# Naming, per engine, only the latest awaited stage, and none twice, in a one-core Mamba and transformer kernel

## The chip, the cores and the metric

The kernel runs on one core of one Trainium2 chip. The metric is the device time of that core in microseconds (us), as the median of the runs shown. Each engine of the core (TensorE, here PE; VectorE, DVE; ScalarE, ACT; GpSimd, POOL; SyncE, SP) takes its own list of instructions in order, and the engines meet through semaphores: an instruction adds to one when it has ended, and another engine waits until it has reached a value.

## The reference, cut to what matters

The input is x[4, 1024, 128]. It goes through a bidirectional Mamba block with a layer norm and a residual, then through a transformer of six layers with local attention (16 heads of 64, windows of 32 tokens, each looking back one window) and a gated feed-forward part, and the first block's sum is added at the end.

```
xc = silu(conv(x @ W_in));  dt = softplus(...);  h = h*exp(dt*A) + dt*xc*B;  y = (h*C).sum + xc*D
per layer:  q,k,v = x @ Wqkv;  q,k normed, scaled, rotated;  x = x + softmax(8*q.k, local) @ v @ Wo
            x = x + (a * gelu(gate)) @ W2 + b2,   a,gate = layernorm(x) @ W1 + b1
```

## The kernel before, in words

The program has two blocks, one after the other. `mamba` (lines 175 to 722) takes 8 sequences (4 batches in 2 directions) with 16 states each; a state's step is a scan on DVE (L658), a product on POOL (L696) and a sum on PE (L439). `transformer` takes 6 layers of 32 tiles of 128 tokens, and 8 chunks of 512 tokens for the feed-forward part, 48 chunks and 192 tiles in all.

In both blocks the order of the work is written out by hand. `PE_ORDER`, `ACT_ORDER`, `DVE_ORDER` and `POOL_ORDER` (and `MAMBA_PE` and its like) list the stages of one iteration as (lag, which tile, name); `sequence` unrolls them, so that each engine has one flat list of (name, k), and a stage is a function that emits the waits and the instructions of one entry. One iteration of the transformer is one chunk with its four tiles. No queue is reordered.

Every stage name has its semaphore in `done`, and `after` (L972 for the transformer, L225 for the Mamba block) puts one wait per producer named, whatever was waited for before:

```python
def after(eng, *producers):
    for name, k in producers:
        eng.wait_ge(done[name], k + 1)
```

So `output` on PE waits for the four stages `copy_mixed0` to `copy_mixed3`, all of them ACT's, and for the reader of the PSUM bank that it takes (`turn_free`), often an ACT stage too; `score` waits for four `copy_heads` and `exponent`, all ACT's; `mix` waits for `turn_probs`, `copy_rows`, the two shift DMAs (`shifted_back`) and the readers of four banks. `ff_added` waits for `x_low` and `x_ready`, which DVE raises one after the other.

The program has 9211 such instructions in the transformer (PE 3203, ACT 3036, DVE 1972, POOL 804, SP 196) and 2013 in the Mamba block (PE 370, ACT 718, DVE 489, POOL 292, SP 144). Stages call first, as a rule, for the data they read (`("normed..")` in `head_turn`, `("square..")` in `squares`, `("sc..")` in `read_out`) and then for the buffer they overwrite.

Other waits are written out with `wait_ge` where they belong to no stage (weights, tables, DMA landings, the steps within a stage).

Of the kernel before, what the change touches and what calls it, by code (L numbers as in the profile page):

```python
# [164 lines left out]
def mamba(nc, xn, resid, c_rows, kept, kept_stored, weights, hbm):  # L165
    win, wtap, wx, wdt, wout, packed, ident, pick, ln, ones_mean, centring, eps_col = weights
    with ExitStack() as ctx:
# [38 lines left out]

        COUNT, done = {}, {}
# [689 lines left out]

def transformer(nc, ctx, consts, xa, xb, resid, kept, kept_stored, hbm, out, stored):
# [72 lines left out]

    def after(eng, *producers):  # L972
        for name, k in producers:
            eng.wait_ge(done[name], k + 1)

    def ff_added(eng, chunk):

        eng.wait_ge(x_low, chunk + 1)
        eng.wait_ge(x_ready, chunk + 1)
# [22 lines left out]
    with nc.Block() as block:  # L1002
        @block.sync
        def _(sp):
# [22 lines left out]
            def load_w2(l):  # L1027
                if l >= 2:
                    ff_added(sp, CHUNKS * l - 1)
                sp.dma_start(w2[:, l % 2], hbm["w2"][l]).then_inc(w2_loaded, 16)  # L1030
                sp.dma_start(lp[:, l % 2], hbm["lp"][l]).then_inc(w2_loaded, 16)
# [42 lines left out]
        def _(pe):  # L1074
# [6 lines left out]
            def in_variance(chunk):  # L1081
                after(pe, ("in_square", chunk))
                bank = turn_free("in_variance", chunk)
                pe.matmul(bank, ones_mean[:, :], in_work(chunk), start=True, stop=True).then_inc(done["in_variance"], 1)

            def turn_free(name, k, i=0):
                last = TURNS[name, k, i][1]
                if last and last[0] == "ff_output":
                    ff_added(pe, CHUNKS + last[1])
                elif last and last[0] in ("fold0", "fold1"):  # L1090
                    pe.wait_ge(vo_copied, 4 * last[1] + 2 * int(last[0] == "fold1") + last[2] + 1)
                elif last and last[0] == "mix":
                    after(pe, (f"copy_mixed{last[2]}", last[1]))
                elif last and last[0] == "in_variance":
                    pe.wait_ge(done["in_rstd"], 2 * last[1] + 1)
                elif last:
                    after(pe, (TURN_READERS[last[0]], last[1]))
                return turn_bank(name, k, i)

            def fold(two):  # L1100
                def stage(l):

                    pe.wait_ge(wvo_loaded, 32 * l + 32)
                    banks = [turn_free(f"fold{two}", l, odd) for odd in range(2)]
# [7 lines left out]
            def project(part):  # L1112
                def stage(tile):
                    l, t, odd = place(tile)
                    after(pe, ("rest", tile))
                    if t == 0:
                        pe.wait_ge(wqk_low, 2 * l + part + 1)
                    if tile == 0:
                        pe.wait_ge(x_ready, 2)
                    if part:  # L1120
                        after(pe, ("cosines0", tile), ("sines0", tile))
                    elif tile:
                        after(pe, ("cosines1", tile - 1), ("sines1", tile - 1))
# [18 lines left out]
            def row_turn(tile):  # L1142
                l, t, odd = place(tile)
                ff_added(pe, CHUNKS * l + t // CHUNK_TILES)
                bank = turn_free("row_turn", tile)
                pe.transpose(bank[:, 0:P], shifted(xa, t * P, P), ident[:, :]).then_inc(done["row_turn"], 1)  # L1146

            def score(tile):
                l, t, odd = place(tile)
                after(pe, ("copy_heads0", tile), ("copy_heads1", tile), ("copy_heads2", tile), ("copy_heads3", tile))  # L1150
                if tile:
                    after(pe, ("exponent", tile - 1))
                else:
                    pe.wait_ge(const_loaded, 64)
                    pe.wait_ge(x_ready, CHUNKS)
# [47 lines left out]
            def mean(chunk):  # L1203
                after(pe, ("add_output", CHUNK_TILES * chunk + CHUNK_TILES - 1))
                bank = turn_free("mean", chunk)
# [3 lines left out]
            def variance(chunk):  # L1209
                after(pe, ("square", chunk))  # L1210
                bank = turn_free("variance", chunk)
                pe.matmul(bank, ones_mean[:, :], work[:, :], start=True, stop=True).then_inc(done["variance"], 1)  # L1212

            def hidden_part(name, first):
                def part(k):
                    lo, m = HIDDEN_PARTS[k]

                    def stage(chunk):
                        after(pe, ("rest_high", chunk))
                        if chunk % CHUNKS == 0:  # L1220
                            pe.wait_ge(w1_low, chunk // CHUNKS + 1)
                        bank = turn_free(f"{name}{k}", chunk)
# [7 lines left out]
            def ff_output(chunk):  # L1230
                after(pe, *[(f"product{k}", chunk) for k in range(3)])
# [3 lines left out]
                bank = turn_free("ff_output", chunk)  # L1235
# [13 lines left out]
        def _(act):  # L1249
# [27 lines left out]
            def round_high(tile):  # L1277
                l, t, odd = place(tile)
                ff_added(act, CHUNKS * l + t // CHUNK_TILES)
                if tile >= 2:  # L1280
                    after(act, ("project1", tile - 2))
                act.copy(xs_parts[:, odd, 0, :], shifted(xa, t * P, P)).then_inc(done["round"], 1)

            def square(part):
                def stage(tile):
                    after(act, (f"project{part}", tile))
                    if part:
                        after(act, ("squares0", tile))
                    elif tile:
                        after(act, ("squares1", tile - 1))  # L1290
# [3 lines left out]
            def inverse_norm(tile):  # L1294
                odd = tile % 2
                after(act, ("guard", tile))
                if tile >= 2:
                    after(act, ("normed0", tile - 2), ("normed1", tile - 2))
# [5 lines left out]
            def copy_heads(c):  # L1304
                def stage(tile):
                    name = f"copy_heads{c}"
                    after(act, (f"head_turn{c}", tile))
                    bank = turn_bank(f"head_turn{c}", tile).rearrange("p (j n) -> p j n", j=4)
                    if tile >= 2:
                        after(act, ("score", tile - 2))  # L1310
# [5 lines left out]
            def copy_rows(tile):  # L1316
                after(act, ("row_turn", tile))
                if tile >= 2:
                    after(act, ("mix", tile - 2))
# [3 lines left out]
            def exponent(tile):  # L1323

                after(act, ("find_max", tile))
                if tile >= 2:
                    after(act, ("turn_probs", tile - 2))
# [5 lines left out]
            def copy_mixed(w):  # L1333
                def stage(tile):
                    after(act, ("mix", tile))
                    if tile >= 2:
# [429 lines left out]
```

## Time and profile before

| what | value |
|---|---|
| median of 3 runs | 3916.18 us (3915.42 to 3918.15) |
| profiled execution, its own time | 3923.24 us |
| its span, first to last instruction | 3921.5 us |
| granted TensorE clock, mean | 0.979 |
| PE busy | 3716.7 us, 95% |
| DVE, POOL, ACT busy | 3307.3, 3178.6, 3035.4 us |

The profile is of one execution. A busy PE means that a matmul was under way by a modelled end. PEld is the weight load of a matmul, which overlaps the matmul before. The event-semaphore instructions are not counted as busy; the view of one source line lists them under PEldq, ACTq, DVEq and so on, where a long one is a wait that it held. "issue" as releaser means that no wait that the profile shows ended the idle time.

### The profile page before, as it was taken

How to read it: one execution, taken by the hardware profiler on the slowest of the kernel's cores; microseconds unless marked ns; L12 is line 12 of the kernel's file. 1: busy time of each engine (PE TensorE's matmuls, PEld its weight loads, DVE VectorE, ACT ScalarE, POOL GpSimd, SP SyncE). 2: the span in 40 equal slices, each digit the busy share in tenths (PEclk: the TensorE clock that was granted, in tenths of full speed). 3: DMA queues.
4: the chain of work that ended last, by engine and by line, in shares of the span. 5: the costliest groups of instructions: out<-in, count | busy, mean ns of one | idle time of the engine just before them, and what ended most of it. 6: DMA issues, size and time to landing. Idle time of an engine off the chain costs nothing.

```text
span 3921.5 us, 115027 instructions
## 1 busy us (share of the span) xinstructions
PE 3716.7 (95%) x45104; PEld 2578.1 (66%) x45104; DVE 3307.3 (84%) x3327; ACT 3035.4 (77%) x7250; POOL 3178.6 (81%) x2370
## 2 busy tenths in 40 slices
PE   7999999988799999999999999999999999999997
PEld 2444444433377777777777777777777777777775
DVE  2999999999688887888878887888878888788885
ACT  7776667666488887888878887888878887888885
POOL 2787778877688888888888888888888888888883
PEclk8999999999899999999999999999999999999999
DMA  1122222222100000000000000000000000000001
GB/s 60 71 81 76 76 74 73 81 73 84 43 21 7 20 7 6 21 7 20 7 10 18 7 20 6 11 17 7 21 6 10 18 7 20 7 11 6 7 7 47
DMA packets 62307, 115.01 MB, mean 29 GB/s; under 512 B 10820, under 2 KB 37320, under 8 KB 61648
## 3 DMA queue, kind: packets, MB, share of 16 engines
q1 hardware_dynamic: 61776, 107.66, 8.3%
q8 instruction: 366, 6.00, 0.6%
q14 instruction: 165, 1.35, 0.1%
HBM read 90.32 MB, written 4.72 MB: 24 GB/s over the span
## 4 chain that ended last, share of the span: by engine, by line
PE 66%; issue 3%; ACT 2%; POOL 1%; DVE 0%; POOLq 0%; ACTq 0%; DVEq 0%
PE ps L1199 17%; PE ps L1127 13%; PE ps L1188 9%; PE ps L1138 8%; PE ps L1175 6%; PE ps L1224 5%; PE ps L1237 3%; PE ps L1160 2%; PE ps L1206 1%; PE ps L1212 1%; PE ps L1146 1%; POOL resid L1604 1%; POOL resid L1626 0%; ACT prob L1329 0%; ACT mixed L1338 0%
## 5 line engine op out<-in xcount | busy, mean ns | idle before, releaser
L1604 POOL TENSOR_TENSOR resid<-resid,sq 128x1024 f32<-128x1024 f32 x384 | 910.3, 2376 | 2.1 <-DVE sq L1459 2.1
L696 POOL TENSOR_TENSOR read<-state,c_row 128x1024 f32<-128x1024 f32 x256 | 646.2, 2540 | 178.7 <-DVE state L658 99.4
L1626 POOL TENSOR_TENSOR resid<-resid,rnorm 128x1024 f32<-128x1024 f32 x384 | 725.0, 1904 | 17.8
L1199 PEld LDWEIGHTS ps<-mixed,w_vo 128*128 128x128 f32 x6144 | 710.9, 193 | 26.7 <-issue 18.6
L1199 PE MATMUL ps<-mixed,w_vo 128*128 128x128 f32 x6144 | 720.2, 276 | 3.2 <-ACT mixed L1338 3.2
L1127 PE MATMUL ps<-w_qk,xs_parts 128*128 128x512 f32 x2304 | 635.6, 412 | 37.4 <-issue 19.4
L1329 ACT ACTIVATE prob<-ps,stat 128x64 f32<-128x64 f32 x3072 | 650.8, 382 | 0.7 <-DVE stat L1479 0.5
L1459 DVE TENSOR_TENSOR sq<-ps,rope_l 128x1024 f32<-128x1024 f32 x384 | 462.5, 1205 | 103.9 <-ACT sq L1291 103.7
L1472 DVE TENSOR_TENSOR resid<-ps,rope_l 128x1024 f32<-128x1024 f32 x384 | 464.9, 1211 | 82.5 <-ACT sq L1291 75.2
L1291 ACT ACTIVATE sq<-ps 128x1024 f32<-128x1024 f32 x384 | 395.6, 1030 | 154.2 <-PE ps L1127 121.4
L1127 PEld LDWEIGHTS ps<-w_qk,xs_parts 128*128 128x128 f32 x2304 | 414.0, 192 | 152.5 <-issue 74.1
L1338 ACT COPY mixed<-ps 128x512 f32<-128x512 f32 x768 | 399.4, 602 | 135.9 <-PE ps L1188 135.7
L439 PE MATMUL mamba_ps<-read,ident 128*128 128x512 f32 x1024 | 498.9, 623 | 3.0 <-POOL read L696 3.0
L1633 POOL TENSOR_TENSOR prob<-prob,stat 128x1024 f32<-128x1024 f32 x192 | 365.7, 1905 | 160.7 <-DVE stat L1490 160.7
L1436 DVE TENSOR_REDUCE ssq<-sq 128x16 f32<-128x1024 f32 x384 | 465.6, 1213 | 5.5 <-ACT sq L1291 0.9
L658 DVE TENSOR_TENSOR_SCAN state<-decay,mamba_ps 128x1024 f32<-128x1024 f32 x192 | 430.5, 2270 | 10.8 <-ACT decay L591 6.0
L1138 PE MATMUL ps<-ident,resid 128*128 128x128 f32 x3072 | 421.4, 276 | 14.6 <-ACT w_vo L1273 13.1
L1138 PEld LDWEIGHTS ps<-ident,resid 128*128 128x128 f32 x3072 | 351.8, 141 | 86.1 <-issue 66.3
L439 PEld LDWEIGHTS mamba_ps<-read,ident 128*128 128x128 f32 x1024 | 190.8, 198 | 230.3 <-issue 219.9
L1313 ACT COPY q_t<-ps 128x512 f32<-128x512 f32 x384 | 234.5, 611 | 117.3 <-PE ps L1138 114.6
L1175 PE MATMUL ps<-k_t,q_t 64*32 64x64 f32 (+1 forms) x24576 | 291.7, 224 | 32.2 <-issue 32.1
L591 ACT ACTIVATE decay<-dt,neg_a 128x1024 f32<-128x1024 f32 x256 | 280.2, 1142 | 49.6 <-DVE state L658 49.4
(149 smaller groups left out, 6038.1 us busy)
## 6 DMA issues: line engine op xcount, KB each, us to landing
c_row<-c_rows SPq DMA_DIRECT2D x128, 512.0 KB, 3.6
rows_back<-rows SPq DMA_DIRECT2D x192, 48.0 KB, 1.9
w_stage<-w_qk_hbm SPq DMA_DIRECT2D x12, 512.0 KB, 4.6
vo_stage<-w_v_hbm SPq DMA_DIRECT2D x6, 512.0 KB, 4.0
vo_stage<-w_o_hbm SPq DMA_DIRECT2D x6, 512.0 KB, 5.0
rows_back<-rows SPq DMA_DIRECT2D x192, 16.0 KB, 1.8
xn<-x_hbm SPq DMA_DIRECT2D x4, 512.0 KB, 5.7
kept<-resid SPq DMA_DIRECT2D x8, 256.0 KB, 4.2
```

The source lines that it names most:

```text
L439: last = pe.matmul(y_ps[h][:, c, :], ident[:, :], read[:, h, g % 2, cols(c)], start=False, stop=n == LAST)
L696: pool.tensor_tensor(read[:, h, g % 2, :], state[:, h, g % 2, :], c_row[:, g % C_AHEAD, :], ALU.mult).then_inc(done[f"rd{h}"], 1)
L1127: last = pe.matmul(ps[:, A + c, :], xs_parts[:, odd, xpart, :], w_qk[:, wpart, cols], start=k == 0, stop=k == 2)
L1138: last = pe.transpose(bank[:, j * P:(j + 1) * P], qk[:, tile % 2, col:col + P], ident[:, :])
L1175: last = pe.matmul(ps[w * WINDOW:(w + 1) * WINDOW, S + h, first:(a + 1) * 2 * WINDOW], q_t[rows_h, odd, a, w * WINDOW:(w + 1) * WINDOW], k ...
L1199: last = pe.matmul(bank[:, 0:P], w_vo[:, l % 2, head_at(place_h), :], mixed[:, odd, place_h, :], start=place_h == 0, stop=place_h == HEADS ...
L1329: last = act.activation(prob[:, tile % 2, place_h, :], score_ps[:, place_h, :], ACT.Exp, bias=stat[:, tile % 2, 0, place_h:place_h + 1])
L1436: dve.tensor_reduce(ssq[:, tile % 2, part * HEADS:(part + 1) * HEADS, 0], sq[:, 0, :].rearrange("p (h d) -> p h d", d=HEAD_DIM), AX_X, ALU ...
L1459: dve.tensor_tensor(sq[:, 1 + part, :].rearrange("p (h s d) -> p h s d", s=2, d=HEAD_DIM // 2), swapped, table(part, 1, tile).rearrange("p ...
L1472: dve.tensor_tensor(qk[:, tile % 2, part * INNER:(part + 1) * INNER].rearrange("p (h d) -> p h d", d=HEAD_DIM), heads_ps.rearrange("p (h d ...
L1604: pool.tensor_tensor(qk[:, tile % 2, cols], qk[:, tile % 2, cols], sq[:, 1 + part, :], ALU.add).then_inc(done[f"rotated{part}"], 1)
L1626: pool.tensor_tensor(heads, heads, norms, ALU.mult).then_inc(done[f"normed{part}"], 1)
```

## The change

One helper, `latest`, gets all stages that a call of `after` names. It keeps, for each engine that produces some of them, the one that stands last in that engine's list, drops it if the waiting engine has already waited for that place or a later one, and notes the place. The stages that are left are waited for in the order PE, ACT, DVE, POOL. Places are looked up in the flat lists.

```diff
+def places(orders):
+    return {stage: (side, n) for side, order in enumerate(orders) for n, stage in enumerate(order)}
+
+def latest(met, eng, stages, places):
+    asked = {}
+    for side, n, stage in sorted((*places[stage], stage) for stage in stages if stage[1] >= 0):
+        asked[side] = n, stage
+    asked = {side: x for side, x in asked.items() if x[0] > met.get((eng.engine, side), -1)}
+    met.update({(eng.engine, side): n for side, (n, _) in asked.items()})
+    return [stage for _, stage in asked.values()]
```

In the Mamba block the calls stay where they are; DMA stages (`cd`, `cst`) are waited for as before, ahead of the others:

```diff
             for name, k in producers:
-                if k >= 0:
+                if k >= 0 and name in ("cd", "cst"):
                     eng.wait_ge(c_spread[k % C_AHEAD] if name == "cd" else done[name], COUNT[name, k])
+            for stage in latest(met, eng, [x for x in producers if x[0] not in ("cd", "cst")], stands):
+                eng.wait_ge(done[stage[0]], COUNT[stage])
```

In the transformer `after` uses `latest` too, `ff_added` goes and is replaced by `after(eng, x_of(chunk))`, which names `in_norm` or `add_ff` and waits for `x_ready` alone, and in each stage on PE, ACT and DVE the separate calls become one (on DVE `cosines` and `add_ff` keep two). A PE stage now puts the bank's reader into the same call:

```diff
-            def turn_free(name, k, i=0):
+            def freed_by(name, k, i=0):
                 last = TURNS[name, k, i][1]
                 if last and last[0] == "ff_output":
-                    ff_added(pe, CHUNKS + last[1])
-                elif last and last[0] in ("fold0", "fold1"):
+                    return [("add_ff", last[1])]
+                if last and last[0] in ("fold0", "fold1"):
                     pe.wait_ge(vo_copied, 4 * last[1] + 2 * int(last[0] == "fold1") + last[2] + 1)
...
+            def turn_free(name, k, *producers):
+                after(pe, *producers, *freed_by(name, k))
+                return turn_bank(name, k)
...
             def head_turn(c):
                 def stage(tile):
-                    after(pe, (f"normed{c // 2}", tile))
-                    bank = turn_free(f"head_turn{c}", tile)
+                    bank = turn_free(f"head_turn{c}", tile, (f"normed{c // 2}", tile))
...
             def mix(tile):
-                after(pe, ("turn_probs", tile), ("copy_rows", tile))
+                after(pe, ("turn_probs", tile), ("copy_rows", tile), *[x for w in range(WINDOWS) for x in freed_by("mix", tile, w)])
                 shifted_back(pe, tile)
-                banks = [turn_free("mix", tile, w) for w in range(WINDOWS)]
+                banks = [turn_bank("mix", tile, w) for w in range(WINDOWS)]
...
             def output(tile):
                 l, t, odd = place(tile)
-                after(pe, *[(f"copy_mixed{w}", tile) for w in range(WINDOWS)])
                 if t == 0:
                     pe.wait_ge(vo_copied, 4 * l + 4)
-                bank = turn_free("output", tile)
+                bank = turn_free("output", tile, *[(f"copy_mixed{w}", tile) for w in range(WINDOWS)])
```

No computing instruction, no DMA, no buffer and no place in an order is changed.

## Rows read from the trace of the kernel before

**Rows 1.** The page: busy time of each engine, share of the span, instructions.
```profile
PE 3716.7 (95%) x45104; PEld 2578.1 (66%) x45104; DVE 3307.3 (84%) x3327; ACT 3035.4 (77%) x7250; POOL 3178.6 (81%) x2370
```

**Rows 2.** Busy us by stretch: PE, PEld, DVE, ACT, POOL; then clock, DMA share, GB/s.
```profile
0.00:1022.00 1022.00, 933.54 (x2658) 422.14 (x2658) 908.47 (x517) 683.78 (x957) 746.83 (x305) 0.95 0.22 75
1022.00:3921.50 2899.50, 2783.13 (x42448) 2155.93 (x42446) 2398.82 (x2810) 2351.58 (x6294) 2431.76 (x2066) 0.99 0.05 13
```

**Rows 3.** View of one line: count, shortest/median/longest ns, first and last start.
```profile
L974 PEldq EVENT_SEMAPHORE  x3111: 51/51/3930, 1033.5 to 3910.6; - x195
...
L974 DVEq EVENT_SEMAPHORE  x1957: 21/21/3454, 1038.6 to 3906.3; - x196
...
L229 PEldq EVENT_SEMAPHORE  x365: 51/51/6463, 19.1 to 1006.2; - x183
```

**Rows 4.** Groups of PE instructions: busy, mean ns, idle before and releasers.
```profile
L1127 PE MATMUL ps<-w_qk,xs_parts 128*128 128x512 f32 x2304 | 635.6, 412 | 37.4 <-issue 19.4 <-DVE sq L1459 8.7 <-DVE resid L1472 8.1
...
L1175 PE MATMUL ps<-k_t,q_t 64*32 64x64 f32 (+1 forms) x24576 | 291.7, 224 | 32.2 <-issue 32.1
```

**Rows 5.** L974 from 1556.5 to 1557 us; timeline of PEld around it.
```profile
L974 PEldq EVENT_SEMAPHORE  x3: 51/51/51, 1556.6 to 1556.8; - x3
...
1556.49 0.28 PEld L1175 LDWEIGHTS ps<-k_t,q_t 64*32 64x32 f32 x26 [1.46 <-issue]
1556.90 0.34 PEld L1188 LDWEIGHTS ps<-prob_t,rows_back 32*128 32x128 f32 x8
```

**Rows 6.** Timeline of PEld, another stage behind `score`, with one such instruction.
```profile
1526.33 1.48 PEld L1175 LDWEIGHTS ps<-k_t,q_t 64*32 64x32 f32 x128
1527.90 1.19 PEld L1224 LDWEIGHTS ps<-ff_parts,w_parts 128*85 128x85 f32 x6
```

**Rows 7.** Timeline around 1541.9 us, and L974 there.
```profile
1541.19 0.62 ACT L1338 COPY mixed<-ps 128x512 f32<-128x512 f32 x1
1541.92 0.14 PEld L1138 LDWEIGHTS ps<-ident,resid 128*128 128x128 f32 x1 [0.16 <-issue]
...
L974 PEldq EVENT_SEMAPHORE  x1: 51/51/51, 1541.8 to 1541.8; - x1
```

**Rows 8.** The same place one iteration later.
```profile
1600.23 0.31 PEld L1138 LDWEIGHTS ps<-ident,resid 128*128 128x128 f32 x3 [0.16 <-issue]
```

**Rows 9.** Timeline of POOL and PEld: a wait that rides on the instruction.
```profile
1159.75 1.27 POOL L1641 TENSOR_TENSOR ff_parts<-xc_ff,ff_parts 128x512 fp32r<-128x512 f32 x1
1161.07 0.93 PEld L1224 LDWEIGHTS ps<-ff_parts,w_parts 128*128 128x128 f32 x3 [2.69 <-POOL ff_parts L1641]
```

**Rows 10.** Timeline of PEld: from `project1` to `mix`.
```profile
1523.83 0.19 PEld L1127 LDWEIGHTS ps<-w_qk,xs_parts 128*128 128x128 f32 x1
1524.37 0.31 PEld L1188 LDWEIGHTS ps<-prob_t,rows_back 32*128 32x128 f32 x8 [0.36 <-issue]
```

**Rows 11.** Timeline of DVE: `squares1` and `guard`.
```profile
1527.92 1.21 DVE L1436 TENSOR_REDUCE ssq<-sq 128x16 f32<-128x1024 f32 x1
1529.21 0.22 DVE L1445 TENSOR_REDUCE floored<-ssq 128x32 f32<-128x64 f32 x1
```

**Rows 12.** Timeline of POOL: the last two steps of `refine`, then `normed0`.
```profile
1576.71 0.24 POOL L1616 TENSOR_TENSOR newton<-three_halves,newton 128x32 f32<-128x32 f32 x1
1577.03 0.25 POOL L1618 TENSOR_TENSOR rnorm<-rnorm,newton 128x32 f32<-128x32 f32 x1
1577.43 1.90 POOL L1626 TENSOR_TENSOR resid<-resid,rnorm 128x1024 f32<-128x1024 f32 x1
```

**Rows 13.** Timeline of the Mamba block: DVE's scan and POOL's product.
```profile
508.99 2.29 DVE L658 TENSOR_TENSOR_SCAN state<-decay,mamba_ps 128x1024 f32<-128x1024 f32 x1
511.35 2.37 POOL L696 TENSOR_TENSOR read<-state,c_row 128x1024 f32<-128x1024 f32 x1 [3.48 <-DVE state L658]
```

**Rows 14.** The view of waits: engine, line, releaser, us in total, times, longest.
```profile
POOL read L696 <- DVE state L658: 99.4, 57, 9.0
...
PEld ps L1127 <- issue: 74.1, 64, 3.8
```

More of the change, by code:

```diff
@@ L204, in mamba @@
         y_ps = [ps[:, 4 + 2 * h:6 + 2 * h, :] for h in range(HALVES)]
+        met, stands = {}, places((PE_SEQ, ACT_SEQ, DVE_SEQ, POOL_SEQ))
         COUNT, done = {}, {}
@@ L970, in transformer, with x_of @@
     KEPT = 16 * CHUNKS
+    met, stands = {}, places((PE_SEQ, ACT_SEQ, DVE_SEQ, POOL_SEQ))
+    done |= {"in_norm": x_ready, "add_ff": x_ready}
     def after(eng, *producers):
[L973 to L979, printed above, removed]
+        for name, k in latest(met, eng, producers, stands):
+            eng.wait_ge(done[name], k + 1 + CHUNKS * int(name == "add_ff"))
+    def x_of(chunk):
+        return ("in_norm", chunk) if chunk < CHUNKS else ("add_ff", chunk - CHUNKS)
     def shifted_back(eng, tile):
@@ L1103, in stage @@
                     pe.wait_ge(wvo_loaded, 32 * l + 32)
-                    banks = [turn_free(f"fold{two}", l, odd) for odd in range(2)]
+                    after(pe, *freed_by(f"fold{two}", l, 0), *freed_by(f"fold{two}", l, 1))
+                    banks = [turn_bank(f"fold{two}", l, odd) for odd in range(2)]
                     for h in range(8 * two, 8 * two + 8):
@@ L1118, in stage @@
                     if tile == 0:
[L1119 to L1123, printed above, removed]
+                        after(pe, ("in_norm", 1))
+                    other = tile if part else tile - 1
+                    after(pe, ("rest", tile), (f"cosines{1 - part}", other), (f"sines{1 - part}", other))
                     for c in range(2):
@@ L1149, in score @@
                 l, t, odd = place(tile)
[L1150 to L1153, printed above, removed]
+                after(pe, ("copy_heads0", tile), ("copy_heads1", tile), ("copy_heads2", tile), ("copy_heads3", tile),
+                      ("exponent", tile - 1))
+                if not tile:
                     pe.wait_ge(const_loaded, 64)
-                    pe.wait_ge(x_ready, CHUNKS)
+                    after(pe, ("in_norm", CHUNKS - 1))
                 for h in range(2):
@@ L1209, in variance @@
             def variance(chunk):
[L1210 to L1211 removed]
+                bank = turn_free("variance", chunk, ("square", chunk))
                 pe.matmul(bank, ones_mean[:, :], work[:, :], start=True, stop=True).then_inc(done["variance"], 1)
@@ L1234, in ff_output @@
                     pe.wait_ge(w2_loaded, 32 * l + 32)
-                bank = turn_free("ff_output", chunk)
+                bank = turn_free("ff_output", chunk, *[(f"product{k}", chunk) for k in range(3)])
                 for k, (lo, m) in enumerate(HIDDEN_PARTS):
@@ L1285, in stage @@
                 def stage(tile):
[L1286 to L1290, printed above, removed]
+                    after(act, (f"project{part}", tile), (f"squares{1 - part}", tile if part else tile - 1))
                     act.activation(sq[:, 0, :], heads_ps, ACT.Square).then_inc(done[f"square{part}"], 1)
@@ L1295, in inverse_norm @@
                 odd = tile % 2
-                after(act, ("guard", tile))
-                if tile >= 2:
-                    after(act, ("normed0", tile - 2), ("normed1", tile - 2))
+                after(act, ("guard", tile), ("normed0", tile - 2), ("normed1", tile - 2))
                 act.activation(rnorm[:, odd, :], floored[:, odd, :], ACT.Ln, scale=float(2 ** NORM_SHIFT)).then_inc(rs_log, 1)
@@ L1306, in stage @@
                     name = f"copy_heads{c}"
-                    after(act, (f"head_turn{c}", tile))
+                    after(act, (f"head_turn{c}", tile), ("score", tile - 2))
                     bank = turn_bank(f"head_turn{c}", tile).rearrange("p (j n) -> p j n", j=4)
-                    if tile >= 2:
-                        after(act, ("score", tile - 2))
                     pairs = slice(4 * (c % 2), 4 * (c % 2) + 4)
@@ L1316, in copy_rows @@
             def copy_rows(tile):
-                after(act, ("row_turn", tile))
+                after(act, ("row_turn", tile), ("mix", tile - 2))
                 if tile >= 2:
-                    after(act, ("mix", tile - 2))
                     shifted_back(act, tile - 1)
@@ L1364, in round_chunk @@
             def round_chunk(chunk):
-                after(act, ("affine", chunk))
-                if chunk:
-                    after(act, *[(f"{name}{k}", chunk - 1) for name in ("gate", "value") for k in range(3)])
+                after(act, ("affine", chunk), *[(f"{name}{k}", chunk - 1) for name in ("gate", "value") for k in range(3)])
                 act.copy(ff_parts[:, 0, :], xc[:, :]).then_inc(done["round_high"], 1)
@@ L1432, in stage @@
                 def stage(tile):
-                    after(dve, (f"square{part}", tile))
-                    if tile >= 2:
-                        after(dve, ("guard", tile - 2))
+                    after(dve, (f"square{part}", tile), ("guard", tile - 2))
                     dve.tensor_reduce(ssq[:, tile % 2, part * HEADS:(part + 1) * HEADS, 0],
@@ L1441, in guard @@
             def guard(tile):
-                after(dve, ("squares0", tile), ("squares1", tile))
-                if tile >= 2:
-                    after(dve, ("refine", tile - 2))
+                after(dve, ("squares0", tile), ("squares1", tile), ("refine", tile - 2))
                 dve.tensor_reduce(floored[:, tile % 2, :], ssq[:, tile % 2, :, :], AX_X, ALU.max).then_inc(done["guard"], 1)
```

60 lines of the change are left out of this document (18 added, 42 removed).

## The prediction

> **What bounds the kernel now.** I read the page first, then the busy time by stretch, the groups of PE instructions, the waits, the view of the line that emits the waits, and the timeline at single places. The page shows PE as the busiest engine, 3716.7 us or 95% of the span, with DVE at 84%, POOL at 81% and ACT at 77% [rows 1]. By stretch there are two regimes. In the transformer, 2899.5 us long, PE is busy for 2783.1 us, so it stands still for 116.4 us, while DVE, POOL and ACT each have about 470 us or more to spare. In the Mamba block, 1022 us, PE (933.5) and DVE (908.5) are close; DVE's scans are slow single instructions and PE's work there hangs on them [rows 2]. So in the transformer time goes only where PE begins a stage sooner, and in the Mamba block where DVE's or PE's chain gets shorter.
>
> The change takes no computing away. What it removes stands in the view of the line: 3111 event-semaphore instructions on PE's queue and 1957 on DVE's in the transformer, 365 on PE's queue in the Mamba block. Their median is 51 ns on PE and 21 ns on DVE; the long ones held a wait [rows 3]. Going along the hand-written lists with the rule of the diff I count, over both blocks, about 3570 falling to about 720 on PE, 3750 to 540 on ACT, 2460 to 460 on DVE, 1100 to 260 on POOL, and nearly none of SP's 340. The question is how many of them stand where the engine has nothing else to do.
>
> **The change part by part.**
>
> *PE, instructions removed.* Taken at the pace of [rows 5] (three of them start within 0.2 us, so one each 0.1 us), 2850 removed instructions would be 285 us. That can't be: PE stands still for 116.4 us in all there. Most are passed while PE still works off matmuls that are queued. The timeline shows it from the side of the weights: `mix` loads its first weights 0.35 us after the last load of `project1` ended (1524.02 to 1524.37), although no releaser is named [rows 10], and that step is about as long wherever I looked at it, with its three instructions passed 0.5 to 1.8 us earlier or just before. I count such steps at nothing: the cover is the queue of matmuls, and without the cover they would cost 0.1 us for each instruction.
>
> Three places are not covered.
>
> (a) `mix` behind `score`. `score` is 128 short matmuls, and PE's queue is nearly empty when it ends. In the first case [rows 5] the last load of `score` ends at 1556.77 and that of `mix` begins at 1556.90, 0.13 us, with three instructions between, the last about 0.08 us ahead of the load. In the second [rows 6] another stage follows `score` with one: 1527.81 to 1527.90, 0.09 us. After the change `mix` keeps one of three (its waits on ACT become one, the one on DVE and the shift DMAs stay). The gain is bounded by 0 and by two times 0.1 us; I take the nearest rows, 0.13 less 0.09, 0.04 us. Once in each of 48 iterations: 1.9 us.
>
> (b) Where the awaited stage is late and its wait stands in a separate instruction. At one such place [rows 7] ACT's copy ends at 1541.81 and PE's load begins at 1541.92, 0.11 us, and the separate instruction stands between, at 1541.8. Elsewhere [rows 9] the awaited wait rides on the instruction itself: POOL ends at 1161.02, the load begins at 1161.07, 0.05 us. After the change the ACT wait is the first of `head_turn1`'s list and rides. 0.06 us, once per iteration ([rows 8] are the same place one iteration on, with the same 0.16 us idle): 48 x 0.06 = 2.9 us.
>
> (c) The same at scattered places. Loads of `project` alone were idle 64 times [rows 14], and there the DVE waits (`cosines`, `sines`) stand in a separate instruction now and come first after. Of these and of the like at `row_turn` and the other `head_turn` stages I take 50 that really waited: 50 x 0.06 = 3.0 us; none and 110 are the bounds, 0 and 6.6 us. The longest of them, 3.8 us, wait for the next layer's weights at the layer's boundary; of those the change takes 0.06 us each and no more. The idle 32.1 us ahead of L1175 and 19.4 us ahead of L1127 [rows 4] have no wait in the profile, and I leave them.
>
> *DVE and POOL in the transformer.* `guard` waits for `squares1` of its own engine in a separate instruction: L1436 ends at 1529.13 and L1445 starts at 1529.21, 0.08 us [rows 11]. `normed0` waits for `refine` in a separate one: 1577.28 to 1577.43, 0.15 us, where the step before it, whose wait rides, takes 0.08 us (1576.95 to 1577.03) [rows 12]. Both come to ride. No row shows the DVE case after; by POOL's and PE's it is 0.05 to 0.07 less. 192 x 0.05 = 9.6 us on DVE and half of 192, 96 x 0.07 = 6.7 us on POOL, 16.3 us together. Both engines have slack [rows 2], so this reaches the end only where PE waits for them. I take 15% of it, 2.5 us; 0 and 8 us are the bounds. Elsewhere on DVE and ACT the separate instruction is passed while the engine is still in the operation before it, one of 1 us or more, and I cost it at nothing.
>
> One of the skill's rules speaks against this part. The Trainium skill, VectorE: DVE Perf Modes, section "The DRAIN you can't avoid", says that copies with a semaphore after each took just as long as with one after the last: there a semaphore costs DVE nothing. By that rule the DVE share of the 2.5 us, about 1.5 us, would fall away. The trace shows a start [rows 11] 0.08 us after the end of the operation awaited, which neither proves nor denies it.
>
> *The Mamba block.* The same removal helps DVE's scans, which wait for their own engine's drive through a separate instruction, and PE and ACT a little: 30 to 40 such places at 0.05 us, 1.8 us. Against it stands the new order of the waits. POOL's product (`read_out`) now has the wait on DVE's scan riding: the scan ends at 511.28 and the product starts at 511.35, 0.07 us [rows 13]. After, the DMA wait rides, and the scan stands behind it in a separate instruction, as `refine` does in [rows 12]: 0.15 us. POOL waited 57 times for the scan [rows 14]: 57 x 0.07 = 4.0 us on POOL, which has 275 us to spare there [rows 2]. Of those I take a fifth on the path, 0.8 us. Behind that waiting product stand POOL's other products and, through the sum on PE, the gate on DVE. Net 1.0 us gained; bounds 3 us gained and 4 us lost.
>
> *Other edits.* `x_low` is no longer waited for, since `x_ready` comes after it on the same engine; no row shows anything that waits for it alone: nothing. SP keeps its waits: nothing. Nothing new is waited for, as each wait that is left is one of those asked before. The bank's reader is asked together with the data; the stage needs both anyway: nothing.
>
> **The sum.** 1.9 + 2.9 + 3.0 + 2.5 + 1.0 = 11.3 us off. The profiled execution took 3923.24 us (span 3921.5 and 1.7 around it), which gives 3911.9. It is 7.1 us above the median of the runs shown, 3916.18, so there I expect 3904.9, rounded 3905.
>
> **The rivals.**
>
> *Hidden anyway.* PE works through its queue, the late ones are late by their data and not by a separate instruction, and what is won at one place is lost at the next, which waits for the same slack engines. For it: the small part of 3570 instructions that I could find uncovered; against it: [rows 7, 9], whose 0.06 us lies behind the data's arrival. It leaves (a) and a part of (b), some 3 us: 3913.
>
> *PE is held up far more often.* If the 82 us that are left of PE's 116.4 us idle in the transformer after the long stalls at layer boundaries (34 us: five of 3.8 us as in [rows 14], ten of some 1.5 us behind the folded weights) were half due to separate instructions, 41 us would go: 3875. For it: the "issue" [rows 4] with no releaser; against it: the timeline [rows 10], where the step is the same with and without a separate instruction just ahead.
>
> *Slower, as the late wait moves off the instruction.* The stages called first for the data they read, and the new order asks PE, ACT, DVE, POOL. Where a stage needs ACT and POOL or the DMA and DVE, the late one now stands in a separate instruction, +0.07 us. The place is POOL's product, 256 of them, in a chain product, sum, scan. If all paid, 256 x 0.07 = 17.9 us, less 8 us won elsewhere: 3926. It decides from 110 of 256 on the path; the waits show 57 that waited at all [rows 14], which speaks against it.
>
> **How the numbers follow.** Forecast 0.55, hidden anyway 0.27, held up far more 0.10, slower 0.08. This kernel's measurement tells 0.2%, 7.8 us, from no change; that is 3908.4 and 3924.0. The forecast's own range is 3896 to 3911, a tenth of it above 3908.4. Faster: 0.50 + 0.10 = 0.60. Same: 0.05 + 0.27 = 0.32. Slower: 0.08. The range for 8 in 10 reaches from the forecast up over the hidden case to 3917 and down part of the way to the large one, to 3888.
>
> **What would show it.** The view of the line should count about 680 on PE's queue instead of 3111 in the transformer. The load of `mix` behind `score` should begin 0.09 us after the last load of `score`, that of L1138 behind ACT's copy 0.05 us after it, `guard` about 0.03 us after `squares1`, `normed0` 0.08 us behind `refine`, and POOL's product 0.15 us behind the scan. PE's idle time in the transformer should fall from 116 us to about 106. It is wrong if that idle time stays, or if it falls by tens, or if the Mamba block's stretch gets longer.

## The result and the profile after

The changed kernel takes 3873.8 us (median of 4 runs, 3869.6 to 3883.8) against 3915.9 of the kernel before on the same chip (4 runs, 3915.4 to 3918.2): a ratio of 0.9895, 95% interval 0.9875 to 0.9915. It is 42 us faster, where 11 were forecast; the time lies below the range of 3888 to 3917. The profiled run of the changed kernel is the slowest of its four, 3883.8 us.

The page of the changed kernel: busy time of each engine, then two of its DMA queues (packets, MB, share).

```profile
PE 3707.5 (96%) x45104; PEld 2569.8 (66%) x45104; DVE 3296.5 (85%) x3327; ACT 3038.9 (78%) x7250; POOL 3180.4 (82%) x2370
...
q8 instruction: 355, 5.82, 0.6%
q14 instruction: 119, 0.97, 0.1%
```

The computing instructions are those of before [rows 1], and each engine's busy time differs by under 12 us. By stretch, cut at the end of the Mamba block as in [rows 2], which comes 5.2 us later here (us; then PE, PEld, DVE, ACT, POOL busy; clock, DMA share, GB/s):

```profile
0.00:1027.20 1027.20, 943.09 (x2656) 425.20 (x2656) 897.71 (x516) 683.61 (x956) 746.79 (x305) 0.94 0.22 75
1027.20:3882.00 2854.80, 2764.38 (x42448) 2144.57 (x42448) 2398.78 (x2812) 2355.32 (x6295) 2433.64 (x2066) 0.99 0.05 13
```

The transformer is 44.7 us shorter than in [rows 2]. PE stands still there for 90.4 us instead of 116.4, and is itself "busy" 18.8 us less with the same matmuls (their ends are modelled, so a short gap between two of them can count as busy). The granted clock is the same, 0.99. The Mamba block took 5.2 us longer in this execution. The lines that emit the waits, as the kernel now has them (count, shortest/median/longest ns, first and last start):

```profile
L995 PEldq EVENT_SEMAPHORE  x485: 51/51/51, 1032.2 to 3871.9; - x162
...
L995 DVEq EVENT_SEMAPHORE  x205: 21/21/21, 1060.1 to 3878.1; - x103
```
```profile
L232 PEldq EVENT_SEMAPHORE  x52: 51/51/51, 19.5 to 980.1; - x52
```

These answer to [rows 3]. With the waits that other lines emit, the transformer has 680 of them on PE, as forecast, where it had 3203 (3111 of those on the one line). None on these lines is long any more. But the wait for the shift DMAs ahead of `mix`, which has a line of its own in the view now, is often long:

```profile
L1003 PEldq EVENT_SEMAPHORE  x192: 51/1263/2851, 1093.0 to 3840.8; - x192
```

The groups that answer to [rows 4]:

```profile
L1148 PE MATMUL ps<-w_qk,xs_parts 128*128 128x512 f32 x2304 | 635.1, 411 | 36.2 <-POOL w_qk L1544 20.0
...
L1193 PE MATMUL ps<-k_t,q_t 64*32 64x64 f32 (+1 forms) x24576 | 284.9, 224 | 8.6 <-issue 8.3
```

Here is most of the surprise. `project` (L1148) has nearly what it had. The matmuls of `score` (L1193) lost 23.6 of 32.2 us of idle time, nearly all of which no wait explained, and 6.8 us of busy time. The same in the view of waits, before and then after (total us, times, longest):

```profile
PE ps L1175 <- issue: 32.1, 44, 2.0
```
```profile
PE ps L1193 <- issue: 8.3, 13, 1.6
```

`score` waits for nothing once it has begun, and yet PE halted 44 times in the middle of one before, and 13 times after. Here is one such `score` of before, from the side of the weights (start, us, group, idle before it):

```profile
1139.34 1.44 PEld L1175 LDWEIGHTS ps<-k_t,q_t 64*32 64x32 f32 x120
1142.22 0.16 PEld L1175 LDWEIGHTS ps<-k_t,q_t 64*32 64x32 f32 x8 [1.45 <-issue]
```

There are 120 loads in 1.44 us, then 1.45 us of nothing, then the last 8. An undisturbed one, of the changed kernel, and the `mix` behind it:

```profile
1552.12 1.50 PEld L1193 LDWEIGHTS ps<-k_t,q_t 64*32 64x32 f32 x128
1553.71 0.31 PEld L1206 LDWEIGHTS ps<-prob_t,rows_back 32*128 32x128 f32 x8
```

Going through the records of all 192 tiles from the first to the last matmul of a stage: `score` took 325.7 us in all before (from the start of its first to the start of its last matmul, summed) and 295.5 after, 30.2 less. The gaps ahead of stages (from the start of the last matmul of one stage to the start of the first of the next) lost 11.5 us (`mix` 4.0, `head_turn1` 2.9, `project0` 2.3, `head_turn0` 1.2, `row_turn` 1.1). The rest of the 44.7 is spread.

### The profile page after: what moved, and what is told of

The parts are those of the page before. It is cut to its first block, busy times and chain, and to the rows that moved or that the text cites. A ratio compares the mean times of both kernels' runs of the same rounds, so it can differ in the third digit from the quotient of the medians.

```text
span 3882.0 us, 106132 instructions
## 1 busy us (share of the span) xinstructions
PE 3707.5 (96%) x45104; PEld 2569.8 (66%) x45104; DVE 3296.5 (85%) x3327; ACT 3038.9 (78%) x7250; POOL 3180.4 (82%) x2370
## 3 DMA queue, kind: packets, MB, share of 16 engines
q8 instruction: 355, 5.82, 0.6%
## 4 chain that ended last, share of the span: by engine, by line
PE 65%; POOL 5%; ACT 1%; DVE 1%; issue 1%; DMA 0%; POOLq 0%; DVEq 0%; SPq 0%
PE ps L1216 16%; PE ps L1148 13%; PE ps L1206 9%; PE ps L1158 8%; PE ps L1193 6%; PE ps L1238 5%; PE ps L1250 3%; POOL resid L1584 2%; PE ps L1178 2%; PE ps L1222 1%; PE ps L1227 1%; POOL prob L1613 1%; POOL resid L1606 1%; POOL w_qk L1544 1%; PE ps L1165 1%
## 5 line engine op out<-in xcount | busy, mean ns | idle before, releaser
L1148 PE MATMUL ps<-w_qk,xs_parts 128*128 128x512 f32 x2304 | 635.1, 411 | 36.2 <-POOL w_qk L1544 20.0
L1148 PEld LDWEIGHTS ps<-w_qk,xs_parts 128*128 128x128 f32 x2304 | 412.4, 191 | 151.6 <-DVE sq L1445 32.1
L1613 POOL TENSOR_TENSOR prob<-prob,stat 128x1024 f32<-128x1024 f32 x192 | 366.3, 1908 | 152.6 <-DVE stat L1474 152.6
L1479 DVE STREAM_TRANSPOSE prob_t<-prob 128x1024 f32<-128x1024 f32 x192 | 238.0, 1240 | 73.4 <-POOL prob L1613 72.0
```

The lines of the kernel that those rows point to most:

```text
L1148: last = pe.matmul(ps[:, A + c, :], xs_parts[:, odd, xpart, :], w_qk[:, wpart, cols], start=k == 0, stop=k == 2)
```

## The theory

The page of the profile gives the clue: the queue of kind "instruction" moved 366 packets before and 355 after. A packet has 16,384 bytes (5.82 MB by 355). PE's stream is 93,781 instructions before (twice 45,104, as a matmul is a load and a multiply, and 3573 semaphore instructions) and 90,949 after; divided by 256 these are 366.3 and 355.3. So q8 carries PE's own program in blocks of 256 instructions of 64 bytes. I numbered that stream from the program and laid it beside the records. If a halt is a step of over 0.4 us from the start of one load of `score` to the start of the next, all 57 halts of the two kernels stand at number 189 or 190 of 256. One `score` is 272 instructions, more than a block, and is issued in 1.5 us. In the stretch around the halt above, in 40 slices of 0.2 us (the window is 1136 to 1144 us), the packet shows in slice 21, from 1140.0 us on:

```profile
DMA  0000000000000000000020000000000000000000
...
q8 instruction: 1, 0.02, 0.7%
```

PE ran out at 1140.78 and went on at 1142.22, some 2 us after that packet began. **Theory A:** PE asks for its next block late, `score` eats the rest of the present one in at most 1.5 us, and PE halts until the new one has come. By this theory it asks late when its sequencer is behind, and each semaphore instruction ahead of `score` keeps it back by 0.1 us [rows 5]. The Trainium skill, Runtime: NRT & Kernel Launch, section "Instruction fetch mechanics", has the sequencer refill its memory in 16 KiB blocks of 256 instructions by its own DMA queue, and the packets here agree. It adds that the cost of a boundary is "mostly hidden"; here the halts left PE idle for 32.1 us in `score` alone. Two forms of it differ in what makes the sequencer late: the number of such instructions (A1), or being held by them (A2). **Theory B**, the rival: earlier releases by the other engines, or the waits at the stage itself, make the gain. **Theory C**: halts belong to certain tiles.

## The experiments

Each kernel was run 4 to 10 times beside the kernel before on its chip. "Halts" is the row that names `issue` ahead of `score`'s matmuls in the view of waits, from the one profile that each kernel has.

| kernel | median us | ratio, 95% | halts, us |
|---|---|---|---|
| before | 3915.9 | 1 | 44, 32.1 |
| changed | 3873.8 | 0.9895 (0.9875 to 0.9915) | 13, 8.3 |
| t_pe_only | 3872.3 | 0.9905 (0.9881 to 0.9928) | 9, 4.8 |
| t_not_pe | 3908.0 | 0.9990 (0.998 to 1.000) | 34, 26.3 |
| t_all | 3875.3 | 0.9905 (0.9882 to 0.9928) | 10, 6.1 |
| m_only | 3916.3 | 1.0012 (0.9999 to 1.0025) | 31, 22.3 |
| b_split | 4000.4 | 1.0224 (1.0209 to 1.0240) | 17, 18.7 |
| a_split | 3953.3 | 1.0107 (1.0087 to 1.0126) | 11, 5.0 |
| pe_dummies | 3891.7 | 0.9944 (0.9922 to 0.9965) | 22, 16.9 |
| score_only | 3895.8 | 0.9958 (0.9943 to 0.9972) | 23, 13.5 |
| score_old | 3887.3 | 0.9918 (0.9898 to 0.9939) | 23, 16.7 |
| score_dummies | 3884.3 | 0.9909 (0.9892 to 0.9925) | 24, 17.5 |
| shift128 | 3922.0 | 1.0011 (1.0001 to 1.0022) | 38, 30.8 |
| merged_mask | 3879.7 | 0.9901 (0.9882 to 0.9919) | 7, 4.0 |

In three groups the kernel before had medians of 3913.6, 3913.5 and 3916.3 us and ranged from 3904.8 to 3927.4; ratios are taken within a group.

**Which engine.** In the transformer's `after`, the engines outside the set ask as before (t_pe_only; t_not_pe has `==`; t_all has no such line; in all three the Mamba block's `after` is the old one):

```
     def after(eng, *producers):
+        if eng.engine != nc.tensor.engine:
+            ...     # every wait of the list, x_low too
+            return
         for name, k in latest(met, eng, producers, stands):
```

> Only TensorE's waits of the transformer go by the new rule (its semaphore instructions fall from 3203 to 680); ScalarE, VectorE, GpSimd and SyncE wait as before there, and the Mamba block waits as before on all engines. Theory A, the halts: the profile of the changed kernel has `score` 30 us shorter from its first to its last matmul over 192 tiles, since TensorE's own stream has fewer instructions; then this kernel keeps nearly the whole gain, 3870 to 3882 us against 3916, and shows 10 to 25 halts of over 0.4 us inside `score` instead of 44. Theory B, the other engines' earlier releases make the gain: 3908 to 3914 us, and 40 or more halts.

> The complement: in the transformer every engine but TensorE goes by the new rule, TensorE keeps all its 3203 semaphore instructions, and the Mamba block is as before. Theory A (halts inside `score` hang on TensorE's own stream): 3911 to 3916 us, which is the guard and normed0 terms alone (2.5 us), with 40 or more halts. Theory B: 3876 to 3890 us, with few halts.

TensorE's waits alone give 41 us, all of the gain as far as the runs can tell; the other four engines together 4 to 6. Both times are near what theory A said (9 halts are one under its 10 to 25, and 34 halts and 3908.0 us under its 40 and 3911), and far from theory B's. The row of each (t_pe_only, then t_not_pe):

```profile
L1198 PE MATMUL ps<-k_t,q_t 64*32 64x64 f32 (+1 forms) x24576 | 284.2, 224 | 5.1 <-issue 4.8
```
```profile
L1198 PE MATMUL ps<-k_t,q_t 64*32 64x64 f32 (+1 forms) x24576 | 290.8, 224 | 26.7 <-issue 26.3
```

Theory B falls as to the engines. In t_not_pe the gaps ahead of `project0`, which waits for DVE and POOL, are 4.7 us shorter (38.6 for 43.3), which is the term that I had at 2.5; in the changed kernel they are 2.3 us shorter.

**The Mamba block.**

> The transformer as in the changed kernel, the Mamba block as before. In the profiled pair the Mamba block ended 5.5 us later with the change. If the new waits of the Mamba block cause that, this kernel is 3 to 6 us faster than the changed kernel, 3866 to 3871 us, and its first transformer project0 starts at about 1027 us. If it was chance of that one execution: 3872 to 3876 us, the same as the changed kernel.

> The Mamba block as in the changed kernel, the transformer as before. If the new waits of the Mamba block cost 5.5 us: 3919 to 3922 us, and project0 of the first tile starts at about 1032 us. If that was chance: 3913 to 3917 us and about 1027 us.

t_all is not faster than the changed kernel, and the transformer began at 1021.3 us in it and at 1019.6 in m_only, against 1027.1 before and 1032.3 in the changed kernel. As m_only has the Mamba block of the changed kernel, the 5 us were chance. The effect of the Mamba block's new waits is too small to tell: m_only is 2.7 us above its group's before, the interval just reaches 1. It has 31 halts by the view, though TensorE's waits in the transformer are untouched there; but 51 of its 192 scores take over 1.6 us, against 49 before and 21 in the changed kernel. So the row of the view alone is a rough count.

**A burst cut in two.** In both kernels, where `mix` stands right ahead of `score`, half of the `score` is put ahead of it:

```
+            split = [n + 1 for n in range(len(order) - 1)
+                     if order[n][0] == "mix" and order[n + 1][0] == "score"]
             for n, (name, k) in enumerate(order):
+                if n + 1 in split:
+                    score(order[n + 1][1], 0)           # masks and pairs 0 to 3
+                stages[name](k, *([1] if n in split else []))
```

> The kernel before, all its waits kept, with one thing moved: where `mix` stands right ahead of `score` in TensorE's order (three of four tiles), the first half of that `score` (its 4 mask matmuls and 4 of 8 pairs, some 140 of its 272 instructions) is issued ahead of the `mix` and the second half behind it. Theory A (every one of the 57 halts seen in before and in the changed kernel stands at one place of TensorE's instruction stream, every 256th instruction, inside a `score`, and ends 2.1 to 2.5 us after the start of a 16384-byte instruction packet: a `score` eats 256 instructions in 1.4 us, and the next 256 are not there yet): without an unbroken burst there are no halts in the three split tiles of four, 8 to 14 halts are left of 44, and the kernel takes 3882 to 3893 us with no wait removed; the half score ahead of `mix` may hide some of its wait too, which would make it less. Theory B (the halts are the price of the waits ahead of `score`, whatever its length): 35 to 45 halts, 3908 to 3920 us. Slower than 3920: `score`'s own waits now hold up `mix`.

> The changed kernel with `score` split around `mix` in the same way. Theory A: 13 halts become 2 to 5 and 7 to 10 us go: 3862 to 3870 us. Theory B: no change, 3870 to 3878 us.

The times are a miss: 87 us slower instead of 20 to 34 faster, and 80 slower than the changed kernel instead of some 8 faster. As to the halts the theory held where the burst was cut: the time lost in halts of more than 0.4 us between two loads fell from 18.3 to 2.8 us in the 142 split tiles, and stayed for the most part (25.4, 20.9) in the 50 others. The row of the table, 17 halts and 11 in a_split, is above the 8 to 14 and the 2 to 5 that I expected. What I had not priced is the rest. In the view of waits of b_split:

```profile
ACT mixed L1349 <- PE ps L1195: 297.7, 192, 5.0
```

ACT waited 135.7 us for the results of `mix` before and 297.7 now. PE itself needs 0.25 us to begin `mix` behind a half `score` and begins the half 0.20 us later than it began `mix`, 142 times; gaps ahead of `row_turn` behind `score` grew from 9.8 to 31.6 us and those of `head_turn1` behind `head_turn0` from 11.2 to 23.0. As an estimate, that is 64, 22 and 12 us more and 20 us of halts less, 78 of the 87. So this cut shows that most halts of `score` go with its unbroken burst, but it is no improvement.

**Number or hold.** The changed kernel with satisfied waits in place of those dropped on PE:

```
+        if eng.engine == nc.tensor.engine:
+            for _ in range(asked - len(chosen)):     # waits before less waits now
+                eng.wait_ge(x_low, 1)
```

> The changed kernel, but for every wait of TensorE that the change drops in the transformer it gets one that is long satisfied (on x_low at 1), so that its semaphore instructions are 3184 again as before (3203) and none of the added ones can hold it up. 
In between: 18 of the 42 us come back, with 9 halts; `score`'s matmuls have 12.0 us more of busy and idle time (288.1 and 17.4 us for 284.9 and 8.6). The gaps ahead of `mix` grew by 6.6 us too. That is neither the 3895 to 3912 us of A1 nor the 3873 to 3882 of A2. So something under half of the gain is the mere number of semaphore instructions (A1). That the rest is PE no longer being held by them (A2) is argued and not shown: in the transformer the separate semaphore instructions held PE for 158 us beyond their 51 ns before (195 long ones), and for 179 us in the changed kernel (144, all at the shift DMAs of L1003). That sum didn't fall; where the holds stand did change.

**Ahead of `score` or elsewhere.** score_only is the kernel before with the new rule in `score` alone; score_old the changed kernel with all five waits of `score`; score_dummies the same, with satisfied ones added:

```
     # score_dummies, in the changed kernel's after()
+        if ... producers[0][0] == "copy_heads0":
+            for _ in range(5 - len(chosen)):
+                eng.wait_ge(x_low, 1)
```

> The kernel before, but `score` alone goes by the new rule on TensorE: 381 semaphore instructions fewer, two ahead of each `score`, every other wait of every engine kept. Theory A1 with the sequencer's last instructions ahead of `score` deciding: a good part of the halts goes, 20 to 32 of 44 are left, 3896 to 3906 us. If the lateness is made further back, by `mix`, `head_turn` and `output`: 38 to 45 halts, 3909 to 3915 us.

> The changed kernel, but `score` asks for the copies of all four head groups and for the last exponent again: 387 semaphore instructions come back, two ahead of each `score`. With score_only (the opposite edit on the kernel before: 17.7 us gained, halts 44 to 23) the two make a table. If what stands ahead of `score` and what stands elsewhere on TensorE add up: 3888 to 3896 us and 25 to 35 halts. If each alone would have been enough to bring TensorE in time: 3874 to 3882 us, 13 to 20 halts.

> As score_old, but the waits that come back ahead of `score` are on a count that is long reached, so they cost the sequencer's time and hold nothing up. If the time of two semaphore instructions is what counts: the same as score_old within 4 us and 3 halts. If being held on the copies of heads is what counts: as the changed kernel, 3870 to 3878 us, 10 to 15 halts.

381 instructions less, two ahead of each `score`, gave 17.7 us and took 21 halts. The opposite edits cost 10 to 14 us and brought 10 and 11 halts. In time the two parts nearly add up: `score`'s waits alone gain 17.7 us and the others alone 29 (score_old), both together 42. In halts they overlap: each alone takes 21 of 44, both together 31. score_dummies equals score_old within 3 us and one halt, so right ahead of `score` it is the two instructions themselves (some 0.2 us) that count, and not what they wait for. My guess for score_old (25 to 35 halts, up to 3896 us) was a little high.

**The place in the stream.** The kernel before with 128 instructions at the start of PE's program:

```
+                for _ in range(256):                # two waits to an instruction
+                    pe.wait_ge(ident_loaded, 16)
                 pe.wait_ge(form_dve, 3)
```

> The kernel before with 128 satisfied semaphore instructions at the very start of TensorE's stream, while it waits for the first loads; everything behind stands half a block of 256 later in the stream and is unchanged. Theory A (halts are tied to a place in the instruction stream): the halts leave the 59 scores that start at 176 to 255 of 256 in the old count (43 of which halted) and go to the 58 that started at 48 to 127, again some 40 of them, all at places 189 and 190 of the new count; the sum stays 38 to 46 us and the time 3908 to 3930 us. Theory C (halts belong to certain tiles, by their neighbours in the order of work): the same tiles halt as before.

This decides. Of the 192 scores 49 were disturbed (longer than 1.6 us) before and 45 now, and not one tile is in both sets. None of the 59 that start at 176 to 255 in the old count is disturbed any more; 41 of the 58 at 48 to 127 are. The tile of the example, shifted, lasts 1.50 us without a break:

```profile
1142.37 1.50 PEld L1177 LDWEIGHTS ps<-k_t,q_t 64*32 64x32 f32 x128
1144.02 0.34 PEld L1190 LDWEIGHTS ps<-prob_t,rows_back 32*128 32x128 f32 x8 [0.15 <-issue]
```

Over the profiles of before, the changed kernel, shift128 and the other eight with an unbroken `score` of 272 instructions (all but the splits and merged_mask) there are 276 halts, every one at number 189 or 190 of its stream. They end 2.17 to 3.0 us after the start of the last packet on q8, 2.47 in the median. The 388 scores that pass the same place of a block without a halt, having begun at 176 or later, pass it 2.18 us or more after the start of the packet that is due there. The cause of the halts is settled by that. What sets the moment at which PE asks isn't; the traces show only that it comes earlier with fewer semaphore instructions: among the scores that begin at 176 or later, the packet due starts less than 0.8 us ahead of the first load, or behind it, in 29 of 59 before, in 13 of 60 in score_only and in 5 of 64 in the changed kernel. Nor are such halts peculiar to `score`: between two loads of `mix` there are steps of over 0.6 us at number 189 or 190 too, 5 before (5.5 us) and 5 in the changed kernel (5.9 us).

**A smaller burst**, as a try at something faster than the changed kernel:

```
                 for h in range(2):
-                    for w in range(WINDOWS):
-                        ... ps[queries, S + h, :] ... [..., queries] ...
+                    pe.matmul(ps[:, S + h, :], sight_rows[rows_h, ..., :], ...)
```

> The changed kernel with the mask of `score` written by 2 matmuls of 128 rows instead of 8 of 32 (same values in the same banks): a `score` is 260 instructions instead of 272. Theory A: fewer scores use up a block (61 start where one can, 52 if 12 fewer instructions count), and a halt is shorter by what 12 instructions take; 8 to 13 halts instead of 13 and 0 to 6 us less, 3867 to 3875 us. Against it: a mask matmul of the full height shares the array less with others; then `score` without a halt gets longer than 1.48 us and the kernel 3875 to 3890 us.

There are 7 halts, one under the 8 to 13 expected, and 346 packets for 88,645 instructions (346.3 blocks). But each undisturbed `score` lasts 1.585 us instead of 1.470, 192 times 0.115 or 22 us. The median is 6 us above that of the changed kernel, in the range that I gave for this case; the runs of the two overlap, so this is not shown to be slower, only not faster. No version here beats the changed kernel; t_pe_only and t_all are level with it.

## Why the prediction was wrong

*The direction and the direct terms were right.* The gaps ahead of stages lost 11.5 us, where the whole sum was 11.3; that this is so near is in part luck, as single terms are off by up to 1.6 us and no run shows the 1.0 of the Mamba block. (a) `mix` behind `score` begins 0.09 us after the last load now, as forecast (1553.62 to 1553.71 above); the gaps of that pair fell by 3.4 us (11.6 to 8.2), 1.9 had been forecast. (b) `head_turn1` behind `head_turn0`: 11.2 to 8.2 us, 3.0 for 2.9. (c) The scattered places: `project0`, `head_turn0` and `row_turn` 4.6 us, for 3.0; the 2.3 of `project0` among them can't be told from the DVE and POOL term, which reaches PE at the same place. The places that I named look as I said. In the changed kernel the view of DVE's and POOL's timeline has, one under the other, `squares1` and `guard`, the last of `refine` and `normed0` (two in one group), and scan and product of the Mamba block:

```profile
1540.38 1.21 DVE L1426 TENSOR_REDUCE ssq<-sq 128x16 f32<-128x1024 f32 x1
...
1541.63 0.22 DVE L1433 TENSOR_REDUCE floored<-ssq 128x32 f32<-128x64 f32 x1
```
```profile
1574.12 0.25 POOL L1598 TENSOR_TENSOR rnorm<-rnorm,newton 128x32 f32<-128x32 f32 x1
1574.45 3.77 POOL L1606 TENSOR_TENSOR resid<-resid,rnorm 128x1024 f32<-128x1024 f32 x2
```
```profile
510.02 2.29 DVE L661 TENSOR_TENSOR_SCAN state<-decay,mamba_ps 128x1024 f32<-128x1024 f32 x1
512.48 2.38 POOL L699 TENSOR_TENSOR read<-state,c_row 128x1024 f32<-128x1024 f32 x1 [3.57 <-DVE state L661]
```

`guard` starts 0.04 us behind `squares1` (forecast 0.03, before 0.08 [rows 11]), `normed0` 0.08 behind `refine` (forecast 0.08, before 0.15 [rows 12]), and the product 0.17 behind the scan (forecast 0.15, before 0.07 [rows 13]). So at this place a wait in an instruction of its own cost DVE 0.04 us. The rule quoted from the Trainium skill (VectorE: DVE Perf Modes, section "The DRAIN you can't avoid") is about a semaphore raised after each operation, and doesn't cover it.

*The step that failed* is the cost of nothing for the instructions removed where matmuls are queued ("I count such steps at nothing"), and with it the sentence "The idle 32.1 us ahead of L1175 and 19.4 us ahead of L1127 have no wait in the profile, and I leave them." L1127's idle time stayed (37.4 us, then 36.2), and the profile after names GpSimd's writing of the weights `w_qk` for 20.0 of it. The 32.1 us were 44 halts within `score`, and the change took 30 us of `score`'s time. "The cover is the queue of matmuls" held for PE's array and not for its sequencer: the array works off the queue, but the packet with the next block starts later when the sequencer has more semaphore instructions to handle (less than 0.8 us ahead of 29 of 59 such scores before, of 5 of 64 now). The row stood in the view of waits with its count of 44 and its longest, 2.0 us. An `issue` of 2 us in the midst of a stage that waits for nothing can't be the time of an instruction, and I should have opened the timeline there. One of the halts even stands in [rows 5], 1.46 us ahead of the last 26 loads of a `score`, where I read only the end of the row. The prediction had named its own sign of being wrong, an idle time that falls by tens: it fell by 26 us, from 116.4 to 90.4.

*The rivals.* "PE is held up far more often" came out at 3875, the measured time, by other means: it halved all of PE's unexplained idle time and put it down to separate instructions at the waits. "For it" I had named just the row that decided. *Hidden anyway* (3913) is refuted by the result itself, and by t_pe_only at 3872. *Slower by the late wait* is real at its place (0.17 us for 0.07), but m_only, 2.7 us above its before, shows no effect clear of noise.

*The range.* Its lower end took the large rival in only in part, with a chance of 0.10. The "issue" rows were an unknown of 51 us that I had bounded at 0 on both sides.

## What to carry to other kernels

Idle time that the profile gives to no releaser, inside a stage that has begun, is to be looked at in the timeline before it is costed at nothing: if it comes in pieces of 0.5 to 2 us, compare the number of PE's instructions, divided by 256, with the packets of the instruction queue. A run of short matmuls that issues over 256 instructions in 1.5 us can outrun the fetch. Separate semaphore instructions on PE ahead of it cost time then, though matmuls are queued (17.7 us for 381 of them in score_only), and are the cheap thing to remove. Breaking the burst by putting another stage in its midst cost more here than the halts (87 us slower).

## What the runs showed of the hardware

- PE's program comes in packets of 256 instructions on one DMA queue; 11 packets fewer for 2832 instructions fewer. Over 11 profiles, no `score` that reached the place late in its block went past it sooner than 2.17 us after the packet due began.
- The halts, counted from 0.4 us up, took as long as 2.3 us. A quarter of the scores before were disturbed, mostly those that start in the last 80 of 256 places (43 of 59, against 6 of the other 133).
- `mix` begins 0.25 us behind a half `score` in b_split, without a wait that would explain it.
- A mask matmul on all 128 rows, two of them, made `score` 0.115 us longer than eight on 32 rows each.
